# Contraction fills of half a PSUM bank at six places of a tile instead of a whole bank at three, diagonals one chunk later

## What is computed

```
dbc = einsum('ble,ce->blc', x, W_dbc)            # to 1 + 64 + 64 columns: delta, B, C
delta, Bm, Cm = split(dbc)
delta = softplus(einsum('blr,er->ble', delta, W_dt) + b_dt)
dA  = exp(delta[..., None] * A)                  # per channel e and state n
dBx = (delta * x)[..., None] * Bm[:, :, None, :]
h[t] = dA[t] * h[t-1] + dBx[t]                   # a scan over t, for 64 x 64 pairs (e, n)
y = einsum('blen,bln->ble', h, Cm) + Dp * x      # the contraction over the 64 states n
```

## Time and profile before

| | us |
|---|---|
| median of three runs | 6798.75 |
| profiled execution, its own time | 6804.28 |
| its span in the profile | 6802.5 |
| DVE busy | 6322.3 (93%) |
| POOL busy | 6080.2 (89%) |
| ACT busy | 4927.0 (72%) |
| PE busy, weight loads apart | 4903.7 (72%) |
| mean granted clock of TensorE | 0.783 |

### The profile page before, as it was taken

How to read it: one execution, slowest core, us unless ns; L and a number is a source line. 1 busy time by engine, 2 the same in 40 slices (tenths; PEclk the granted TensorE clock), 3 DMA queues, 4 the chain that set the end, 5 groups by cost and what they waited for, 6 DMA issues and landing times. The chain is left out here.

```text
span 6802.5 us, 114118 instructions
## 1 busy us (share of the span) xinstructions
PE 4903.7 (72%) x32336; PEld 1829.8 (27%) x32336; DVE 6322.3 (93%) x4435; ACT 4927.0 (72%) x10217; POOL 6080.2 (89%) x1940
## 2 busy tenths in 40 slices
PE   5777777777777777777777777677777777774777
PEld 1222222222222222222222222222222222222443
DVE  8999999999999999999999999999999999995554
ACT  6777777777777777777777777777777777772111
POOL 8999999999999999999999999999999999993110
PEclk8777777778777777778778787877777777776888
DMA  6777777777777777777777777777777777772000
GB/s 231 255 250 253 250 256 254 244 252 259 251 253 255 256 255 252 247 251 257 253 255 254 255 254 252 249 253 256 253 253 254 258 250 251 249 248 83 5 7 7
DMA packets 559826, 1561.16 MB, mean 229 GB/s; under 512 B 171938, under 2 KB 317858, under 8 KB 559586
## 3 DMA queue, kind: packets, MB, share of 16 engines
q1 hardware_dynamic: 559714, 1559.89, 68.9%
HBM read 1468.97 MB, written 90.59 MB: 229 GB/s over the span
## 5 line engine op out<-in xcount | busy, mean ns | idle before, releaser
L649 POOL TENSOR_TENSOR u<-dxb,Bt 128x1488 f32<-128x1488 f32 x1792 | 5909.1, 3342 | 134.0 <-DMA dxb<-dx_rows 129.3
L577 DVE TENSOR_TENSOR_SCAN hT<-decay,u 128x744 f32<-128x744 f32 x3584 | 5808.3, 1684 | 138.4 <-ACT decay L409 124.3
L409 ACT ACTIVATE decay<-decay,a_neg 128x371 f32<-128x371 f32 (+2 forms) x7168 | 3632.0, 556 | 652.7 <-PE decay L294 623.4
L294 PE MATMUL decay<-stk,spread 96*128 96x371 bf16 (+2 forms) x7168 | 2152.3, 394 | 1662.6 <-DVE hT L577 1628.2
L312 PE MATMUL z_bank<-hT,Cst 128*32 128x256 f32 x21504 | 1941.3, 493 | 7.6 <-ACT z_sb L418 4.1
L294 PEld LDWEIGHTS decay<-stk,spread 96*128 96x128 bf16 x7168 | 470.2, 104 | 3427.5 <-DVE hT L577 2821.7
L418 ACT COPY z_sb<-z_bank 128x512 f32<-128x512 f32 x1344 | 805.5, 599 | 643.2 <-PE z_bank L312 628.8
L312 PEld LDWEIGHTS z_bank<-hT,Cst 128*32 128x32 f32 x21504 | 664.6, 130 | 972.1 <-issue 770.0
L1092 POOL TENSOR_TENSOR wr<-pr 128x744 f32<-128x744 f32 x8 | 14.1, 1760 | 437.4 <-DVE pr L1015 437.4
L910 ACT ACTIVATE relu<-PB,c_b 128x744 f32<-128x744 f32 x64 | 56.4, 881 | 232.6 <-PE PB L788 232.6
L352 PE MATMUL prep_bank<-tmap,yT 64*128 64x32 f32 (+3 forms) x1344 | 212.6, 295 | 0.0
(11 more groups left out here) (151 smaller groups left out, 2217.0 us busy)
## 6 DMA issues: line engine op xcount, KB each, us to landing
dxb<-dx_rows SPq DMA_DIRECT2D x3584, 372.0 KB, 4.4
delta_parts<-parts SPq DMA_DIRECT2D x112, 279.0 KB, 5.8
stk<-delta_parts SPq DMA_DIRECT2D x112, 279.0 KB, 3.1
y_rows<-z_sb SPq DMA_DIRECT2D x1792, 12.0 KB
yT<-y_rows SPq DMA_DIRECT2D x112, 192.0 KB, 3.3
dx_rows<-dx SPq DMA_DIRECT2D x112, 186.0 KB, 2.3
xT<-in_x SPq DMA_DIRECT2D x64, 186.0 KB, 4.8
xP<-in_x SPq DMA_DIRECT2D x64, 186.0 KB, 4.5
```

The source lines that it names most:

```text
L294: nc.tensor.matmul(slot[:, e, :, 1:], spread[0:PARTS * QR, TILES_G * q + er // TILES_G, :], src[:, er % TILES_G, :, 1:], start=True, stop= ...
L409: last = nc.scalar.activation(bank, bank, ACT.Exp, scale=a_neg[:, l, c:c + 1])
L577: nc.vector.tensor_tensor_scan(hT[q % 2][:, i * PAIR:(i + 1) * PAIR], pair_slot(p), u[c % U_RING][:, part * PAIR:(part + 1) * PAIR], 0.0, ...
L649: tt(u[c % U_RING][:, :].rearrange(channels, t=W0), dxb[slot][:, :].rearrange(channels, t=W0), Bt[buf][:, :].unsqueeze(1).broadcast_to([P, ...
```

## The change

A fill now writes 256 columns, half the bank, with four matmuls, and there are six of them for a tile, at positions 2 to 7. Each has its own copy of 128x256. The matmuls, their columns and what they read are the same in number. A fill waits for the copy before it, as it did. The counts that others wait for follow, since `FILLS` is now 6. The diagonals stand after the broadcasts of chunks 6 to 13; `load_yT` stands after the store of delta's parts at chunk 14.

```
-FILLS = KB // 2
+FILLS = KB
...
-                    if 5 <= c < 13 and prev:
-                        for t in range(2 * (c - 5), 2 * (c - 4)):
+                    if 6 <= c < 14 and prev:
+                        for t in range(2 * (c - 6), 2 * (c - 5)):
                             diagonal(prev, 1 - half, t)
                     if c == 13 and after:
                         store_dx(after, 1 - half)
-                    if c == 13 and prev:
-                        load_yT(prev)
                     if c == 14 and after:
                         store_parts(after)
+                    if c == 14 and prev:
+                        load_yT(prev)
...
-                for kk in range(2):
-                    for g in range(CG):
-                        t0 = TB * (CG * (2 * i + kk) + g)
...
-                        last = nc.tensor.matmul(zb[TB * 2 * g:TB * 2 * (g + 1), kk * EPT * TB:(kk + 1) * EPT * TB],
...
+                for g in range(CG):
+                    t0 = TB * (CG * i + g)
...
+                    last = nc.tensor.matmul(zb[TB * 2 * g:TB * 2 * (g + 1), 0:EPT * TB],
...
-                    if i in (2, 4, 6):
+                    if i >= 2:
                         if q:
-                            fill(here, half, q - 1, i // 2 - 1)
+                            fill(here, half, q - 1, i - 2)
...
-                nc.scalar.copy(z_sb[buf][:, 2 * i:2 * i + 2, :, q * EPT:(q + 1) * EPT], src).then_inc(s_zev, 1)
+                nc.scalar.copy(z_sb[buf][:, i, :, q * EPT:(q + 1) * EPT], src).then_inc(s_zev, 1)
```

More of the change, by code:

```diff
@@ L307, in fill @@
                     pe.wait_ge(s_zev, f)
-                for kk in range(2):
-                    for g in range(CG):
-                        t0 = TB * (CG * (2 * i + kk) + g)
-                        h = hT[q % 2][:, t0:t0 + EPT * W0].rearrange("p (e t) -> p e t", t=W0)[:, :, 0:TB]
-                        last = nc.tensor.matmul(zb[TB * 2 * g:TB * 2 * (g + 1), kk * EPT * TB:(kk + 1) * EPT * TB],
-                                                Cst[buf][:, CG * (2 * i + kk) + g, :, :], h,
-                                                start=True, stop=True, tile_position=(0, 2 * TB * g))
+                for g in range(CG):
+                    t0 = TB * (CG * i + g)
+                    h = hT[q % 2][:, t0:t0 + EPT * W0].rearrange("p (e t) -> p e t", t=W0)[:, :, 0:TB]
+                    last = nc.tensor.matmul(zb[TB * 2 * g:TB * 2 * (g + 1), 0:EPT * TB],
+                                            Cst[buf][:, CG * i + g, :, :], h,
+                                            start=True, stop=True, tile_position=(0, 2 * TB * g))
                 last.then_inc(s_z, 1)
@@ L360, in body @@
                     q, i = divmod(p, TPAIRS)
-                    if i in (2, 4, 6):
+                    if i >= 2:
                         if q:
-                            fill(here, half, q - 1, i // 2 - 1)
+                            fill(here, half, q - 1, i - 2)
                         elif prev:
-                            fill(prev, 1 - half, TILES_G - 1, i // 2 - 1)
+                            fill(prev, 1 - half, TILES_G - 1, i - 2)
                     if after and p in (1, 19, 23):
@@ L416, in read_z @@
                     act.wait_ge(s_diag, 16 * TB * (n - 1))
-                src = zb[:, :].rearrange("p (k e t) -> p k t e", k=2, e=EPT)
-                nc.scalar.copy(z_sb[buf][:, 2 * i:2 * i + 2, :, q * EPT:(q + 1) * EPT], src).then_inc(s_zev, 1)
+                src = zb[:, 0:EPT * TB].rearrange("p (e t) -> p t e", e=EPT)
+                nc.scalar.copy(z_sb[buf][:, i, :, q * EPT:(q + 1) * EPT], src).then_inc(s_zev, 1)
             def take_dt(at):
@@ L501, in body @@
                     q, i = divmod(p, TPAIRS)
-                    if i in (2, 4, 6):
+                    if i >= 2:
                         if q:
-                            read_z(here, half, q - 1, i // 2 - 1)
+                            read_z(here, half, q - 1, i - 2)
                         elif prev:
-                            read_z(prev, 1 - half, TILES_G - 1, i // 2 - 1)
+                            read_z(prev, 1 - half, TILES_G - 1, i - 2)
                     if prev and p == 31:
```

## The result

The changed kernel took 6927.53 us (median of 4 runs, 6918.74 to 6938.84) against 6804.18 for the kernel before in the same rounds: a ratio of 1.0177, interval 1.0149 to 1.0205, so 120 us slower. Forecast were 6760 and at most 6812. The profiled execution has a span of 6937.0 us for 6802.5, and a mean granted clock of 0.773 for 0.783.

A forecast was written before the change was run, and what follows sets the result against it. DVE's scans back to back plus 1.11 us a group of waiting for ACT's decays were the bound; 112 x (-0.34 - 0.18 + 0.16) = -40, +1.4, so -39 us: 6760, range 6680 to 6812 (8 in 10, slow cases left out).

The forecast's parts named there:

- its share of chance for slower, 0.20: Chance of a slower result: 0.17 for PE at the lower clock as bound, 0.03 for diagonals not arriving in time.
- Place 3: DVE's wait for the decay at place 3 goes: 0.39 less 0.05 given back, 0.34 us a group; bounds 0 and 0.39.
- the stall moves: Rival, chance 0.18: the 0.34 comes back at places 4 to 7 or at `t_one`; 6785 to 6810 us.
- Places 26 to 30: Cost of more splits on PE, place 30 0.4 us late in two of five groups: 0.16 us; bounds 0 and 0.6.
- as many fill columns ahead of the spreads of places 28 and 30 as before: Step on PE's order at places 26 to 30: fill columns unchanged there, only the extra splits cost, 0.6 us before place 30.
- The clock: PE's clock low for less time, a quarter of the 0.72 us of waits elsewhere goes: 0.18 us; bounds minus 0.18 and 0.72.
- The last rival: PE at the lower clock is the bound, chance 0.17: half-fill places take 1.76 us against a scan's 1.62; around 6855 us.
- Its other tile: In the lower-clock rival, the tile behind the group's start, said to have no slack for about 1 us more a tile.
- The page that spoke against it: Skill page on PSUM pauses moving PE's clock up and down; by it, no 0.18 gain and the lower-clock rival's loss.
- Diagonals and yT: Later diagonals and yT load: yT lands near 2865, place 27 comes at about 2867; nothing, or PE waits there if late.
- The tail: Behind the last group six half fills and copies run with nothing beside them: 1.4 us more, once.
- POOL's wait below 60 us: Sign in the profile after: POOL's wait for the broadcast dxb, 129.3 us before, falls below 60 us.

The follow-up runs named there:

- hinted changed kernel: The changed kernel with a hint ahead of ACT's back edge that names the loop's head as wanted again: 6828.55 us, ratio 1.0005.
- hinted kernel before: The kernel before with the same hint at ACT's back edges and nothing else: 6803.66 us, ratio 0.9978.
- the run of its own: The kernel before, ACT's loops aligned, with only the diagonals and the load of yT one chunk later: 6807.7 us, ratio 0.9976.
- the fastest kernel: The changed kernel with all fills halved, the hint, and `to_channels` in four parts at places 27 to 30: 6716.99 us, ratio 0.986.
- in the slowest: The kernel before, ACT's loops aligned, with half fills for the third tile alone (places 26 to 31): 7016.91 us, ratio 1.0288.
- the runs at 392 and 404: The changed kernel, ACT's loops aligned: at 392 with one wait for both halves at places 8 to 13, 6889.25 us; at 404 without that, 6897.07 us.

## Why the prediction was wrong

**A term was missing: ACT's code.** The sum counted 24 more copies in a turn only by their time on the engine. Their 48 instructions (a wait and a copy each) took the loop from 356 to 404, past its room. That is 117 us, the second pause at place 1 included; the fills add 18 (below), and the few long pauses of the kernel before, which its own hint takes away, are 15 to its debit (0.9978): 120. The kernel before, begun at another offset, loses as much with its fills untouched. None of the rivals held it. So the result is slower for a reason that no part of the text gives, and its share of chance for slower, 0.20, was for other things.

**The rest of the sum, without the pause.** The hinted changed kernel against the hinted kernel before is 1.0005 to 0.9978, some +18 us where I had -39. (The stalls below come from one profiled execution each, the slowest of ten of the one and the fastest of ten of the other, 44 us apart, so they make the difference too large.)

- *Place 3, forecast 0.34 us a group less.* The mechanism was right: nothing is left of that stall, and with place 2 and 4 the gain is 0.51 us (0.66 to 0.15), above the bound of 0.39, since place 2's went too. Copies of 0.40 us, 2688 of them, came as 397 ns and 2688, and the half fill of 1.01 us at the low clock as 1.01 (2912.44 to 2913.45). (By the counts in the earlier trace rows the 0.43 us are four of a fill's sixteen instructions, not four column groups; four times 0.43 for a fill is right.) But it is no gain by itself: with halves at places 2 to 7 alone it came back at 2 and 4 (0.9967 for 0.9970), the rival "the stall moves" in small.
- *Places 26 to 30, forecast 0.16, bounds 0 to 0.6.* This is the term that failed: 0.79 us (0.54 to 1.33), above the upper bound. The step at fault is "as many fill columns ahead of the spreads of places 28 and 30 as before". It counted from the start of the tile, and it priced the work at one clock. In the changed kernel PE still waits for DVE ahead of the spread of place 27 (0.52 us on average), and the half fill that the change moves from place 26 to 27 stands behind that wait. With it PE takes 1.4 us longer from place 27 to 30 at the upper clock (4.79 to 6.22), which costs nothing, and 1.8 longer below 0.70 (7.30 to 9.08), where the stall is 2.78 us a group for 1.50. And with the hint in both, 51 groups were below 0.70 there for 37. No run moved that half fill alone, so its part can't be told from that of the clock. The second part of `to_channels`, 8 matmuls at one place, I had not costed at all; in four parts, with the half fill where it is, the stall is 0.05.
- *The clock, forecast -0.18.* The mean went from 0.783 to 0.773, and to 0.782 with the pause gone: no gain of that sort. But the idea was right in a form that I had not given it. Half fills at places 18 to 23 keep the clock at 0.75 and more at place 25, whole ones leave it at 0.50 to 0.55 (0.70 in the kernel with halves at 2 to 7), and the same half fills at 26 to 31 cost 1.25 or 2.73 us of stall by that, the same whole fills 0.03 or 0.54. The last of these, 0.51 us, is the gain by the clock that I had forecast at 0.18; the changed kernel loses it again to its halves at 26 to 31. The last rival, the loss at the lower clock, is what half of the groups show at 28 to 31, and it names the right price (its place of 1.76 us at 1.2 GHz is the 1.75 between the spreads at 2911.70 and 2913.45), though its 6855 would be for a kernel without the pause, which came to 6828.55. Its other tile, behind the group's start, did not pay.
- *The page that spoke against it.* The Trainium skill (TensorE: Matmul & The Clock Gate, section "A second HAM failure mode: psum-queue depth-cycling") says that pauses between groups of PSUM work make the clock go up and down. In the stretch above PE had no pause and was at 0.50, and a kernel with as many exchanges between fill and copy as any here, and short `to_channels` blocks, had 1.00 there. These rows don't show the rule at work.
- *Diagonals and yT: nothing.* Right, by the run of its own. *The tail: +1.4 us.* From the last scan to the end the trace has 637.0 us before and 637.9 after; in the other traces it is 633 to 642, so a term of this size can't be seen.
- *POOL's wait below 60 us.* It was 200.4; in the fastest kernel it is 34.0, in the slowest 310.8. It goes up and down with DVE's stalls, which the profile puts down to the decays and not to POOL.

**What stays open.** Why one group runs its places 27 to 29 at the lower clock and the next does not; why the clock stays there in the kernel with halves at 26 to 31 alone, while PE has no pause; and why a shorter end of the group goes with a lower clock at places 0 to 2 of the next (with whole fills, that takes back all that the four parts gave). These are shown as they are, not explained. Nor do I know whether the pause itself adds to the stall at 28 to 31: with the kernel before at offset 200 it rose (0.50 to 1.24, with 56 groups below 0.70 for 33), but it hardly moved when the changed kernel lost its pause (1.31 to 1.33, 51 groups for 50).

The change was worth making all the same: with the hint and four parts of `to_channels` its half fills give 0.986, where the whole fills with both give 0.9977. That is 1.2%, or 80 us, which the code of the loop and one block of PE's had hidden.

## To carry to other kernels

Before adding instructions to an engine's loop, count the body as the engine sees it, waits included, and read the queue that loads instructions: where it has a few packets for each turn (here 281 to 294 in 50 turns, for 44 to 69), the loop doesn't fit, whatever the engine's busy time says. A stall once a turn that the profile blames on an engine which had ended earlier can be that. When small work is moved by one place, count from the last point at which its engine waited, not from the start of the tile, and price it at both levels of the clock: here the same work cost 0.04 us a group at the upper level and 2.78 below 0.70.

## What was not expected of the hardware

- A loop of ScalarE that begins at the start of a block of 256 instructions had no long pause at 356, 368 and 380 instructions (0.23 us, 46 to 51 packets) and had one at 392 (2.62 us, 287). The Trainium skill (Advanced Engine Details and Errata, section "ISA Cache") gives two lines of 256 instructions; by these two lines all of the aligned loops up to 512 would fit, and the runs at 392 and 404 didn't. The measurement decides: with the loop's head at the start of a block, the room ends between 380 and 392. Why there is not shown.
- The same loop costs 0.26 us a turn or 3.8 us by its offset alone (356 instructions, offset 200 in a block): 139 us for the whole kernel between the two placings (6801.06 and 6939.96).
- A hint at the back edge took the pause of 404 instructions from 2.45 to 0.21 us, and cost nothing that could be measured in the kernel that hardly needed it (0.9978 with it, 0.997 aligned without).
- With the third tile's fills halved a kernel took 1.0288, with those of the second as well 1.0077: the granted clock was low in 90 groups of 109 or in 44, and that weighed more than the work of the splits.
